# Four edits to the three last layers of a graph network: a stretched chain, two fused steps, conversions begun earlier, and reciprocal roots on GpSimd

## What is computed

```python
for l in range(3):
    msg = h[src] + h_edge_attr
    agg = segment_sum(msg, dst, 6250)
    out = agg + h
    z = layernorm(out @ W1[l].T + b1[l], g1[l], be1[l])
    z = gelu(z)
    z = layernorm(z @ W2[l].T + b2[l], g2[l], be2[l])
    h = gelu(z + h)
return x + h
```

## Time and profile before

| | us |
|---|---|
| median of 3 runs (lowest to highest) | 4795.1 (4792.8 to 4796.32) |
| the profiled execution | 4790.99 |
| its span in the trace | 4789.2 |
| last product ahead of the layers (L1858) starts | 3679.27 |
| first product of the layers (L1942) starts | 3694.87 |
| PE busy, share of the span | 86% |
| DVE busy | 62% |
| ACT busy | 40% |
| POOL busy | 41% |

### The profile page before, as it was taken

How to read it: one execution, slowest core, us unless ns; L and a number is a source line. 1 busy time by engine, 2 the same in 40 slices (tenths; PEclk the granted TensorE clock), 3 DMA queues, 4 the chain that set the end, 5 groups by cost and what they waited for, 6 DMA issues and landing times.

```text
span 4789.2 us, 100505 instructions
## 1 busy us (share of the span) xinstructions
PE 4136.8 (86%) x35231; PEld 3732.0 (78%) x35231; DVE 2971.1 (62%) x8078; ACT 1933.8 (40%) x4188; POOL 1971.2 (41%) x2199
## 2 busy tenths in 40 slices
PE   1599999999976788888888888888888998998997
PEld 1499999999965677777878778778777777777776
DVE  7799999999933344444444444444445667777676
ACT  1565565565531222222222222222214665666664
POOL 5511111111037777777777777777770000000000
PEclk9799999999989899999999999999999999999999
DMA  5444444444455567667667667767677776776875
GB/s 119 173 205 205 201 201 201 201 211 211 209 164 138 149 196 214 203 198 210 201 199 213 198 202 210 201 202 212 201 196 256 230 232 202 233 230 205 257 236 152
DMA packets 793921, 967.67 MB, mean 202 GB/s; under 512 B 124439, under 2 KB 674055, under 8 KB 781143
## 3 DMA queue, kind: packets, MB, share of 16 engines
q1 hardware_dynamic: 623488, 764.12, 47.4%
q0 software_dynamic: 60048, 125.37, 10.4%
q10 hardware_dynamic: 110151, 75.61, 6.2%
HBM read 707.25 MB, written 257.60 MB: 201 GB/s over the span
## 4 chain that ended last, share of the span: by engine, by line
PE 35%; POOL 35%; issue 15%; DVE 11%; DMA 3%; ACT 1%; POOLq 0%; ACTq 0%; DVEq 0%
POOL ACC L1047 33%; PE ps L1573 9%; PE ps L1942 7%; PE ps L1943 6%; PE ps L1557 4%; PE ps L1559 4%; DMA ACC<-table,BIG 2%; DVE T L2219 2%; DVE BIG L2219 2%; DVE COUNTS L2640 2%; PE ps L1858 1%; POOL ACC L971 1%; DVE ST L2682 1%; PE ps L1960 1%; PE ps L1978 1%
## 5 line engine op out<-in xcount | busy, mean ns | idle before, releaser
L1047 POOL DMA_INDIRECT ACC<-table,BIG x1715 | 1680.5, 980 | 626.2 <-issue 513.7
L1843 PE MATMUL ps<-BIG 128*128 128x257 f32 x3430 | 860.1, 394 | 146.5 <-ACT BIG L1248 145.9
L2462 DVE TENSOR_TENSOR BIG<-ps,ACC 128x512 f32<-128x512 f32 (+1 forms) x441 | 297.9, 676 | 1096.9 <-DMA ACC<-table,BIG 905.2
L1843 PEld LDWEIGHTS ps<-BIG 128*128 128x128 f32 x3430 | 635.3, 196 | 248.0 <-ACT BIG L1248 169.9
L1248 ACT ACTIVATE BIG<-BIG 128x512 f32<-128x512 f32 (+1 forms) x441 | 273.7, 621 | 1321.4 <-DVE BIG L2462 1309.8
L1573 PE MATMUL ps<-H,ACC 128*128 128x128 f32 x4802 | 690.4, 285 | 0.0
L1464 ACT ACTIVATE COUNTS<-X 128x512 fp32r<-128x512 bf16 (+1 forms) x1092 | 599.3, 598 | 147.4 <-PE ps L1943 141.1
L1573 PEld LDWEIGHTS ps<-H,ACC 128*128 128x128 f32 x4802 | 588.2, 192 | 0.2 <-ACT ACC L1189 0.2
L1189 ACT ACTIVATE BIG<-ps 128x392 bf16<-128x392 f32 x784 | 390.1, 498 | 468.2 <-PE ps L1559 468.2
L1942 PE MATMUL ps<-COUNTS,H_BIG 128*128 128x512 f32 (+1 forms) x1274 | 511.7, 402 | 57.9 <-DVE COUNTS L2640 38.1
L1943 PE MATMUL ps<-COUNTS,H_BIG 128*128 128x512 f32 (+1 forms) x1274 | 488.8, 384 | 0.0
(11 more groups left out here) (290 smaller groups left out, 7594.1 us busy)
## 6 DMA issues: line engine op xcount, KB each, us to landing
X<-count_mat SPq DMA_DIRECT2D x360, 512.0 KB, 4.8
weight_mat<-ACC SPq DMA_DIRECT2D x49, 3136.0 KB, 9.2
BIG<-in_edge_attr SPq DMA_DIRECT2D x392, 256.0 KB
count_mat<-BIG SPq DMA_DIRECT2D x49, 1568.0 KB, 12.8
REL_WT<-weight_mat SPq DMA_DIRECT2D x275, 256.0 KB
BIG<-rel_tab ACTq DMA_DIRECT2D x392, 128.0 KB
BIG<-weight_mat SPq DMA_DIRECT2D x176, 256.0 KB
X<-count_mat SPq DMA_DIRECT2D x108, 384.0 KB, 3.5
```

Of the source, the lines that this page charges most:

```text
L1047: pool.indirect_dma_start(GR[:, q * QUAD + u, :], None, tables[1], bass.IndirectOffsetOnAxis(ap=STEP_IDX[:, b % 3, r * QUAD + u:r * QUAD + ...
L1843: mm = pe.matmul(PS[4 + par][:, 0:HIW], DR[:, q * QUAD + u, :], HB[:, q * QUAD + u, :], start=(r == 0 and u == 0), stop=(r == QB - 1 and u ...
L2462: dve.tensor_tensor(HB[:, steps, 0:F], PS[n % 2][:, 0:size * F].rearrange("p (u f) -> p u f", f=F), GR[:, own, :], ALU.add).then_inc(rows_ ...
```

## The change

1. **Roots on GpSimd.** `root_guess` and `root_step` are gone from DVE. GpSimd's `root` waits for a group's moments and does fourteen instructions, each of which waits for the one before it through a semaphore (`then`); the last signals `z_rstd` or `y_rstd`, for which DVE's `z_norm` and `y_add` wait.
2. **Fused.** Three steps of y (normalise, scale, add: four instructions, one, one) become two: `y_center` computes (y - mean) * g2 without the root, and `y_add` multiplies by the root and adds `h`, each with one instruction per block.
3. **Chain spread.** New lags: moments at 13 and the normalisation at 21 for z (12 and 18 before), moments at 36 and `y_add` at 45 for y (33 and 43 before); all later steps move by 2 or 3.
4. **Early conversions.** Items 0 to 6 are converted within `final_chunks`.
5. **Loads and sums.** SP issues the loads of `X_LAST` twice per group from the last layer's first group on; GpSimd does the sums between its roots, from the fifth group of the last layer on.

```diff
+EARLY_ITEMS = {C1 - 3: (0, 1), C1 - 2: (2, 3), C1 - 1: (4, 5, 6)}
-LAG_OF = {"sum_turned": 4, "z": 5, "z_bias": 9, "z_stats": 10, "z_moments": 12, "z_guess": 14, "z_root1": 15, "z_root2": 16, "z_root3": 17, "z_norm": 18,
-          "z_turned": 20, "z_gelu": 23, "y": 25, "y_bias": 29, "y_stats": 31, "y_moments": 33, "y_guess": 34, "y_root1": 35, "y_root2": 36,
-          "y_root3": 37, "y_norm": 39, "y_scale": 41, "y_add": 43, "out": 45, "high": 46, "low": 48}
+LAG_OF = {"sum_turned": 4, "z": 5, "z_bias": 9, "z_stats": 11, "z_moments": 13, "z_norm": 21, "z_turned": 23, "z_gelu": 26, "y": 28,
+          "y_bias": 32, "y_stats": 34, "y_moments": 36, "y_center": 38, "y_add": 45, "out": 47, "high": 48, "low": 50}
...
-                    if l == LAYERS - 1 and s < 7 and k == PIECES_OF_SB - 1:
+                    if l == LAYERS - 1 and s < 4 and k in (6, PIECES_OF_SB - 1) and (s, k) != (0, 6):
+                        first = (s * 2 - (k == 6)) * 7
...
+                def then(ins):
+                    ins.then_inc(root_step, 1)
+                    root_steps[0] += 1
+                    pool.wait_ge(root_step, root_steps[0])
+                def root(g, k, moments, ready):
+                    cols = slice(k, k + of_sb(g)[1])
+                    pool.wait_ge(moments, g + 1)
+                    then(pool.tensor_scalar(nmr[:, cols], MV[:, cols, 1], EPS, None, ALU.add))
+                    then(pool.tensor_scalar(rstd[:, cols].bitcast(I32), nmr[:, cols].bitcast(I32), -0.5, float(0x5f3759df), ALU.mult, ALU.add))
+                    for n in range(3):
+                        then(pool.tensor_tensor(rcnt[:, cols], rstd[:, cols], rstd[:, cols], ALU.mult))
+                        then(pool.tensor_tensor(rcnt[:, cols], rcnt[:, cols], nmr[:, cols], ALU.mult))
+                        then(pool.tensor_scalar(rcnt[:, cols], rcnt[:, cols], -0.5, 1.5, ALU.mult, ALU.add))
+                        last = pool.tensor_tensor(rstd[:, cols], rstd[:, cols], rcnt[:, cols], ALU.mult)
+                        if n < 2:
+                            then(last)
+                    last.then_inc(ready, 1)
...
+                for g in range(SB_COUNT):
+                    l, s = g // SBS, g % SBS
+                    root(g, 0, z_aggr, z_rstd)
+                    if l == LAYERS - 1 and s >= 4:
+                        if s == 4:
+                            pool.wait_ge(x_stored_in, STORED + 14 * 16)
+                        for v in (2 * s - 8, 2 * s - 7) if s < 7 else (s - 1,):
+                            sum_out(l * SBS + v)
+                    root(g, 4, y_aggr, y_rstd)
+                sum_out(SB_COUNT - 1)
...
+            def z_norm(g):
                 l, nb, own = of_sb(g)
-                stepped(name + "_root3", g)
+                dve.wait_ge(z_rstd, g + 1)
                 for j in range(nb):
-                    ins = dve.tensor_scalar(SB_ZY[:, j, :], SB_ZY[:, j, :], MV[:, k + j, 0:1], rstd[:, k + j:k + j + 1], ALU.subtract, ALU.mult)
-                return ins
+                    ins = dve.tensor_scalar(SB_ZY[:, j, :], SB_ZY[:, j, :], MV[:, j, 0:1], rstd[:, j:j + 1], ALU.subtract, ALU.mult)
+                ins.then_inc(zn_ready, 1)
-            def y_scale(g):
+            def y_center(g):
                 l, nb, own = of_sb(g)
-                stepped("y_norm", g)
-                step("y_scale", g, dve.tensor_tensor(SB_ZY[:, 0:nb, :], SB_ZY[:, 0:nb, :], over_nodes(L_G2[l], nb), ALU.mult))
+                dve.wait_ge(y_aggr, g + 1)
+                for j in range(nb):
+                    ins = dve.scalar_tensor_tensor(SB_ZY[:, j, :], SB_ZY[:, j, :], MV[:, 4 + j, 0:1], L_G2[l], ALU.subtract, ALU.mult)
+                step("y_center", g, ins)
             def y_add(g):
...
-                stepped("y_scale", g)
+                stepped("y_center", g)
                 stepped("shift", g)
-                dve.tensor_tensor(H[:, own, :], SB_ZY[:, 0:nb, :], H[:, own, :], ALU.add).then_inc(yn_ready, 1)
+                dve.wait_ge(y_rstd, g + 1)
+                for j in range(nb):
+                    b = own.start + j
+                    ins = dve.scalar_tensor_tensor(H[:, b, :], SB_ZY[:, j, :], rstd[:, 4 + j:5 + j], H[:, b, :], ALU.mult, ALU.add)
+                ins.then_inc(yn_ready, 1)
```

More of the change, by code:

```diff
@@ L1374, in block_support, with converted, early_counts @@
                 act.activation(T1[:, b, :], PS[2][:, 0:P], ACT.Copy).then_inc(node_free, 1)
+            def converted(i):
+                act.wait_ge(raw_in[ITEMS[i][3] % RAWS], RAW_IN0[ITEMS[i][3] % RAWS] + 16 * (ITEMS[i][3] // RAWS + 1))
+                if i >= CSLOTS:
+                    act.wait_ge(counts_used, i - CSLOTS + 1)
+                act.activation(slot_counts(i), raw_counts(i), ACT.Copy).then_inc(act_converted, 1)
+            def early_counts(t):
+                if t == min(EARLY_ITEMS):
+                    act.wait_ge(onehot_ready, QN)
+                    act.wait_ge(group_summed, GROUPS0 + len(GROUPS_OF))
+                for i in EARLY_ITEMS.get(t, ()):
+                    if i % CSLOTS in CSLOTS_OF_ACT:
+                        converted(i)
             def final_chunks():
@@ L2528, in block_scale, with converted, early_counts @@
                 dve.scalar_tensor_tensor(nmr[:, own], MV[:, b, 0:1], -1.0, rstd[:, own], ALU.mult, ALU.mult).then_inc(xn_norm, 1)
+            def converted(i):
+                dve.wait_ge(raw_in[ITEMS[i][3] % RAWS], RAW_IN0[ITEMS[i][3] % RAWS] + 16 * (ITEMS[i][3] // RAWS + 1))
+                if i >= CSLOTS:
+                    dve.wait_ge(counts_used, i - CSLOTS + 1)
+                dve.tensor_copy(slot_counts(i), raw_counts(i)).then_inc(dve_converted, 1)
+            def early_counts(t):
+                if t == min(EARLY_ITEMS):
+                    dve.wait_ge(group_summed, GROUPS0 + len(GROUPS_OF))
+                for i in EARLY_ITEMS.get(t, ()):
+                    if i % CSLOTS not in CSLOTS_OF_ACT:
+                        converted(i)
             def final_chunks():
@@ L2733, in dense_layers @@
             def dense_layers():
-                dve.wait_ge(group_summed, GROUPS0 + len(GROUPS_OF))
                 for pos in range(LAYER_END):
-                    if pos < len(ITEMS) and pos % CSLOTS not in CSLOTS_OF_ACT:
+                    if CSLOTS <= pos < len(ITEMS) and pos % CSLOTS not in CSLOTS_OF_ACT:
                         converted(pos)
@@ L2744, in dense_layers @@
                     for g in behind(pos, "z_moments"):
[L2745 to L2750 removed]
+                        sb_moments(g, "z", 0, z_aggr)
                     for g in behind(pos, "z_norm"):
[L2752 removed]
+                        z_norm(g)
                     for g in behind(pos, "y_bias"):
@@ L2757, in dense_layers @@
                     for g in behind(pos, "y_moments"):
-                        sb_moments(g, "y", 4)
-                    for g in behind(pos, "y_guess"):
-                        root_guess(g, "y", 4)
-                    for n in range(1, 4):
-                        for g in behind(pos, f"y_root{n}"):
-                            root_step(g, "y", 4, n)
-                    for g in behind(pos, "y_norm"):
-                        step("y_norm", g, sb_norm(g, "y", 4))
-                    for g in behind(pos, "y_scale"):
-                        y_scale(g)
+                        sb_moments(g, "y", 4, y_aggr)
+                    for g in behind(pos, "y_center"):
+                        y_center(g)
                     for g in behind(pos, "y_add"):
```

51 lines of the change are left out of this document (9 added, 42 removed).

## The result

| | before | after |
|---|---|---|
| median, us (lowest to highest) | 4793.95 (4789.49 to 4796.32), 4 runs | 4844.15 (4828.07 to 4847.23), 4 runs |
| ratio, with its 95% interval | | 1.0099 [1.0075, 1.0123] |
| span of the profiled execution, us | 4789.2 | 4845.3 |
| last item starts, us | 4762.9 | 4815.8 |

The change makes the kernel **slower by 50 us**, 1.0%. Forecast were 4865 and slower; the sign and the place are right, and sizes behind them are not.

A forecast was written before the change was run, and what follows sets the result against it. PE was taken as busiest, losing time to late DVE conversions. Terms 58 + 19 + 4.9 - 3.5 - 5.7 = +73 us on 4791.0 give 4864, stated as a median of 4865; own range 4815 to 4920, overall range 4735 to 4920.

The forecast's parts named there:

- What bounds it: In the layers PE is busiest at full clock; the change decides when the conversion behind DVE's waiting step comes.
- A step of 0.36 us: Each dependent GpSimd root instruction: 0.19 us plus 0.175 handover; fourteen take 5.1 us, between 3.9 and 7.0.
- Conversions and GpSimd in each other's way: DVE's conversions and y_center beside a root delay GpSimd's steps: 0.4 us added to z, 0.8 us to y.
- held up in full: Rival: each conversion and y_center beside a root costs it that instruction's whole time; 61 us more, 4925; chance 0.13.
- A group loses 5.1 us in place of 2.35: PE's loss per group, z 3.0 and y 2.1 us: +2.75 in 21 groups, +58 us.
- the rounding: Single or paired GpSimd sums between roots delay a conversion by a few tenths in nine groups; not counted.
- the five sums in a row: Five GpSimd sums at once that held up DVE and PE for 4.32 us go, with the slow clock behind: -5.7.
- the other chains: The other 17 chains beside items lose +1.1 us each, between 0 and 2.75: +19 us.
- the edges: Last group's chain +4.9 us, earlier items at the start -3.5, five sums at once gone -5.7.
- Short steps: Rival: a GpSimd step below about 0.29 us gains; 4769 at 0.28, 4713 at 0.20; chance of faster 0.28, about 4755.
- the clock's term: Extra beside "held up in full": low clock behind every other 3 us PE gap, 20 x 1.4 = 28 us on top.

The follow-up runs named there:

- the shorter root: The change with two refinements of the root on GpSimd in place of three, against the kernel before: 4738.01 us, ratio 0.9893.
- the run with longer cover: The change with z's normalisation at place 26, y_add at 53 and chains at least 46 places apart, against the kernel before: 4691.69 us, 0.9790.

## Why the prediction was right or wrong

**What bounds it: right.** DVE idles ahead of its normalisation with GpSimd as releaser, and PE waits for the conversion behind it.

**A step of 0.36 us: wrong.** It is 0.28, which the prediction itself had named as a sign of being wrong. The instruction was well read (0.19 forecast, where its own rows give 0.20; 0.197 us in the mean of 667 steps with no DVE instruction beside them), the handover was not: the earlier trace rows gave 0.19 us of idle time for another instruction with another wait, I took 0.175, and 180 steps of one line show 0.08:

```profile
L1120 POOL TENSOR_TENSOR rstd<-rstd,rcnt 128x4 f32<-128x4 f32 x180 | 42.0, 233 | 15.0
```

**Conversions and GpSimd in each other's way: right.** 14 x 0.28 = 3.9 us; in the group shown the root of z is there 4.4 us after the moments, that of y 4.7: +0.5 and +0.8, where I added 0.4 and 0.8. The Trainium skill, page "SBUF — State Buffer", section "Who interferes with whom", says that a VectorE copy or cast in a two-port mode has the shared pair of ports for its whole instruction, and that a VectorE instruction with two inputs in SBUF contends with a GpSimd instruction that reads SBUF. The conversions of 512 columns agree: the first step of z's root, which falls among them, takes 0.59 to 0.97 us where a free one takes 0.23. Those of 384 columns do not delay a step (0.201 us in 99 steps). For `y_center`, which has two such inputs, the measurement differs from the page: 102 steps beside it alone took 0.201 us, hardly more than free ones, and only the first step of a root is longer beside it (0.38 us in 33 roots with the places of before). So the rival "held up in full" (4925) did not come.

**A group loses 5.1 us in place of 2.35: size wrong, in opposite directions.** Without a fall of the clock it loses 6.7 - 3.6 = 3.1 us, of which 1.85 at place 22 and 1.0 at places 47 and 48. The step's price accounts for that (14 x 0.08 = 1.1 us less in each of the two roots). So +0.85 us instead of +2.75. Two things that the sum does not have then come on top: the clock, which I named beside a rival and left out (some 12 us in the second layer's seven regular groups), and GpSimd's sums with the falls behind them, which I put into the rounding (some 16 us in five groups of the third layer). Against them stand 5.9 us for the five sums in a row that are gone. The 21 regular groups lose 7.82 us in the mean, 5.96 before: +39 us for my 58 - 5.7. With the other chains, from item 64 to the last item, it is +53.4 for 58 + 19 - 5.7 = 71.

**How much of it was luck.** With 0.28 us for a step and its own terms for the conversions the sum gives z 1.9 us and y 1.0, 2.9 in place of 2.35: 21 x 0.55 = 12, some 4 for the other chains, and -6.5 at the edges (4.9 - 2.2 for the tail, -3.5, -5.7): +9, a median of about 4804, which is no change. The clock and the sums, which were not in it, brought the time to 4844. That the forecast of 4865 is 21 us away is in part two errors that cancel. (Its own addition, 4864 and 4.1 for the median, gives 4868.)

**"Short steps": its condition held, its time did not.** At 0.28 us I had 4769: z loses 1.6 us, y 0.3. That was worked out with no conversion in the way. With 3.9 us for the root (14 x 0.28, where the rival has 4.1) and the 0.4 and 0.8 us that I gave to the conversions elsewhere it is about the 1.9 and 1.0 of above, which the trace shows (1.85 and 1.0), and the time would have been near that of before. The clock and the sums make it slower. So what failed besides the step's price is the clock's term: 28 us of it, 1.4 a fall, stood beside a rival as an extra, for gaps of 3 us; it came at gaps of 2, at some 1.6 a fall.

**The edges.** The tail: +4.9 forecast; from the last item's start to the end 26.24 us before and 29.56 after, +3.3, by the same cheaper step. The start: -3.5 forecast, 45.9 - 42.5 = -3.4 measured, but by the branch, not by the early place. The first products of the layers on PE, with their waits in brackets:

```profile
3685.31 0.47 PE L1980 MATMUL ps<-COUNTS,H_BIG 128*128 128x512 f32 x1 [1.98 <-issue]
...
3688.32 0.80 PE L1980 MATMUL ps<-COUNTS,H_BIG 128*128 128x512 f32 x1 [1.85 <-ACT COUNTS L1412]
...
3692.72 0.77 PE L1980 MATMUL ps<-COUNTS,H_BIG 128*128 128x512 f32 x1 [2.32 <-ACT COUNTS L1412]
```

The first starts at 3685, as forecast, and then PE waits for one conversion after the other. The five sums in a row are gone, but single and paired sums, which I put into the rounding, leave five of the last layer's groups 2.5 to 4.5 us longer than the two without sums (8.5 to 10.5 us lost, where those lose 6.0): the sums start exactly when a root is done, on the one DVE instruction for which everything waits.

**What I did not price:** the spread of the chain. I took fusion and spread to lie beside PE; with the roots on VectorE the spread is worth 38 us, the fusion some 4.

Open: whether the falls of the clock alone explain the spread of the change's runs (4828 to 4847) was not tried; the 4828 run has the higher mean granted clock, 0.953 against 0.949. Over 4830 us that is 19 us of full clock more, by estimate as much as the two are apart.

## What to carry to other kernels

A chain that goes to a slower engine costs nothing if the step that takes it back stands far enough behind, and much if it doesn't: price it as latency against places, and move the waiting step before judging the engine. An instruction that waits on an in-order engine is as dear as what is queued behind it; put the wait behind the conversions that PE needs next. And a gap of some 2 us on PE can cost nearly as much again through the clock (1.6 us a fall here), so a removed gap may give back more than its length.

## What the runs showed of the hardware

- In the change the granted clock fell to 0.50 at place 22 in all seven regular groups of the second layer, whose items of that place are 2.0 to 2.3 us late, and in none of the first layer's, where they are 1.85 us late; with items 0.7 to 0.9 us late (the shorter root) it did not fall in either layer. The length of the gap does not decide alone: with the second layer's items 2.0 to 2.3 us late it fell in three of the seven with the sums behind y's root, and in one of the seven, 2.0 us late, without the early conversions; before the change it fell behind items 1.2 us late in the first group of three blocks of two layers and not in that of the other. The Trainium skill, page "TensorE: Matmul & The Clock Gate", section "HAM oscillation — how this bites in real kernels", describes a kernel whose every piece of work starts at the low clock behind a wait; here it is all regular groups of one layer and none of another, and the same group of the second layer falls in one run and not in another.
- GpSimd's instructions on 128 x 4 start 0.28 us apart when each waits for the one before it through a semaphore. Beside DVE's conversions of 512 columns they start 0.44 us apart in the mean (0.37 in the run with longer cover), beside those of 384 columns 0.28, as if free. The conversions of 512 columns took 0.415 us with and 0.420 without such a step beside them: the small steps are delayed, not the long ones.
- The other way round, two GpSimd sums of 512 columns held a normalisation and a `y_add` of DVE (four instructions on 128 x 128) up for 1.9 us each.
